# Non-local attention block: a fourth tile of each image turned by DMA, split by ScalarE and VectorE, and three operand moves made ScalarE copies

## The reference

```python
g     = (einsum('bchw,oc->bhwo', x, w_g) + b_g).reshape(B, N, 64)
theta = (einsum('bchw,oc->bhwo', x, w_theta) + b_theta).reshape(B, N, 64)
phi   = (einsum('bchw,oc->bohw', x, w_phi) + b_phi).reshape(B, 64, N)
att   = softmax(einsum('bnc,bcm->bnm', theta, phi), axis=-1)      # 1024 x 1024 per image
y     = einsum('bnm,bmc->bnc', att, g).reshape(B, H, W, 64)
out   = einsum('bhwc,oc->bohw', y, w_out) + b_out
inv   = bn_gamma / sqrt(bn_var + 1e-5)
return x + out * inv + (bn_beta - bn_mean * inv)
```

## Time and profile before

| | before |
|---|---|
| median of three runs | 206.3 us |
| the profiled execution: its own time | 205.01 us |
| its span | 203.2 us |
| granted TensorE clock over the span | 0.997 |
| share of the span busy: TensorE matmul | 96% |
| VectorE | 86% |
| GpSimd | 76% |
| ScalarE | 67% |
| share of the 16 DMA engines' time, SyncE's queue | 81.3% |

### The profile page before, as it was taken

The page is one execution under the profiler, slowest core; times in us unless marked ns, Lnnn a source line. Parts: engine busy times, 40 slices in busy tenths (PEclk is TensorE's granted clock), DMA queues, the critical chain, the costliest instruction groups (busy, mean ns, idle before and its releaser), DMA issues.

```text
span 203.2 us, 3990 instructions
## 1 busy us (share of the span) xinstructions
PE 195.2 (96%) x1100; PEld 133.6 (66%) x1100; DVE 174.8 (86%) x289; ACT 136.8 (67%) x245; POOL 154.2 (76%) x130
## 2 busy tenths in 40 slices
PE   7998899999999999999999999999999998999993
PEld 7485776587666857677566957677566956566551
DVE  0687989988997899978998899978998899989881
ACT  2679867767486766866577765866577675767731
POOL 2479579999778999699987999699988964954300
PEclk9999999999999999999999999999999999999998
DMA  5309946799999998899979998899988998848102
GB/s 154 98 7 225 240 85 117 167 248 185 188 219 250 222 169 221 187 224 187 233 159 259 230 191 194 168 249 203 198 180 182 226 169 182 132 81 155 52 3 103
DMA packets 59500, 35.28 MB, mean 174 GB/s; under 512 B 50400, under 2 KB 50912, under 8 KB 59488
## 3 DMA queue, kind: packets, MB, share of 16 engines
q1 hardware_dynamic: 59200, 35.01, 81.3%
q10 hardware_dynamic: 288, 0.14, 0.2%
HBM read 8.36 MB, written 4.23 MB: 62 GB/s over the span
## 4 chain that ended last, share of the span: by engine, by line
PE 71%; DVE 10%; DMA 5%; POOL 5%; SPq 4%; issue 3%; ACT 1%; ACTq 0%; DVEq 0%; POOLq 0%
PE ps_scores L757 21%; PE ps_flip L821 12%; PE ps_y L769 11%; PE ps_misc L783 6%; PE ps_y L776 5%; PE ps_misc L741 5%; DVE neg_max L622 4%; PE ps_misc L864 4%; DMA pt_hi<-p_hi 3%; DVE pt_lo L663 3%; SPq L302 2%; POOL p_lo L478 2%; DMA w_tp<-w_tp_t_dram 2%; PE ps_scores L795 1%; POOL x_lo L492 1%
## 5 line engine op out<-in xcount | busy, mean ns | idle before, releaser
L552 ACT ACTIVATE probs<-ps_scores,neg_max 128x1024 f32<-128x1024 f32 x64 | 71.7, 1120 | 29.1 <-DVE neg_max L627 14.9
L622 DVE TENSOR_REDUCE neg_max<-ps_scores 128x1 f32<-128x1024 f32 x64 | 77.9, 1217 | 9.5 <-PE ps_scores L757 9.1
L663 DVE SCALAR_TENSOR_TENSOR pt_lo<-ps_flip,pt_hi 128x512 f16<-128x512 f32 x84 | 54.0, 684 | 5.2 <-ACT pt_hi L539 5.1
L539 ACT ACTIVATE pt_hi<-ps_flip 128x512 f16<-128x512 f32 x84 | 45.6, 595 | 15.2 <-PE ps_flip L821 15.2
L478 POOL TENSOR_TENSOR p_lo<-probs,p_hi 128x1024 f16<-128x1024 f32 x22 | 47.0, 2139 | 4.7 <-POOL p_hi L471 3.9
L757 PE MATMUL ps_scores<-phi_hh,theta_hl 128*128 128x512 f32 x128 | 47.0, 448 | 0.8 <-ACT probs L552 0.6
L821 PE MATMUL ps_flip<-ident,probs 128*128 128x128 f32 x336 | 44.6, 275 | 1.8 <-DVE pt_lo L663 1.0
L821 PEld LDWEIGHTS ps_flip<-ident,probs 128*128 128x128 f32 x336 | 38.1, 142 | 11.1 <-issue 3.6
L757 PE MATMUL ps_scores<-phi_ll,theta_hl 128*128 128x512 f32 x128 | 40.1, 394 | 0.0
L769 PE MATMUL ps_y<-pt_hi,g_parts 128*128 128x512 f16 x120 | 28.4, 379 | 0.1
L757 PEld LDWEIGHTS ps_scores<-phi_ll,theta_hl 128*128 128x128 f32 x128 | 24.0, 188 | 5.6
(11 more groups left out here) (77 smaller groups left out, 173.8 us busy)
## 6 DMA issues: line engine op xcount, KB each, us to landing
x_in<-x_in_dram SPq DMA_DIRECT2D x16, 256.0 KB, 3.3
inv_all<-inv_row SPq DMA_DIRECT2D x15, 256.0 KB, 3.9
out_dram<-resid SPq DMA_DIRECT2D x15, 256.0 KB, 2.7
phi_hh<-hi SPq DMA_DIRECT2D x14, 256.0 KB, 5.7
phi_ll<-lo SPq DMA_DIRECT2D x14, 256.0 KB, 6.2
theta_hl<-hi SPq DMA_DIRECT2D x7, 256.0 KB, 4.7
theta_hl<-lo SPq DMA_DIRECT2D x7, 256.0 KB, 5.5
pt_hi<-p_hi SPq DMA_TRANSPOSE x22, 4.1
```

The lines of the kernel that those rows point to most:

```text
L539: nc.scalar.activation(pt_hi[ring][:, c * HALF_TILES:(c + 1) * HALF_TILES, slot * P:(slot + 1) * P], ps_flip[c][:, :].rearrange("p (a n) - ...
L552: nc.scalar.activation(probs[k % PROB_RING][:, :], ps_scores[k % 2][:, :], ACT.Exp, bias=neg_max[:, k % STEPS:k % STEPS + 1], accum_out=ro ...
L622: nc.vector.tensor_reduce(out=top, in_=ps_scores[k % 2][:, :], op=ALU.max, axis=AX.X, negate=True).then_inc(row_max_ready if by_dma(it, k) ...
L663: nc.vector.scalar_tensor_tensor(out=pt_lo[ring][where], in0=ps_flip[c][:, :].rearrange("p (a n) -> p a n", n=P), scalar=PROB_SCALE, in1=p ...
```

## The change

Tile 2 of every image goes by DMA as well. It does not take GpSimd: ScalarE writes its `p_hi` (`own_high`, in step 3, ahead of exp of tile 3) and VectorE its `p_lo` (`own_low`, in step 3, ahead of the maximum of tile 4). VectorE also adds log(2^15) to that tile's maximum. The reciprocals of the first half now have two scaled columns (places 1 and 2; in the first image 0 and 2). The three moves that keep their partitions become ScalarE copies of 64x1024 (`same_rows`, in steps 4, 6 and 7), counted by a new semaphore `copied`, for which scores of a new image and the overwrite of `hi` now wait.

```diff
-    STACKS = 6
+    STACKS = 3
+    COPIES = 3
+    COPY_STEPS = (4, 6, 7)
...
-    BY_DMA = (1, 5, 7)
+    BY_POOL = (1, 5, 7)
+    BY_ACT = 2
+    BY_DMA = (1, BY_ACT, 5, 7)
...
-    FIRST_BY_DMA = (0, 5, 7)
+    FIRST_BY_POOL = (0, 5, 7)
+    FIRST_BY_DMA = (0, BY_ACT, 5, 7)
...
                     sp.wait_ge(hi_ready, b + 1)
-                    restack(theta_hl[1 - r], 0, hi, 0, 1 - r)
                     restack(phi_hh[1 - r], 0, hi, CI, 1 - r)
-                    restack(phi_hh[1 - r], CI, hi, CI, 1 - r)
+                turn_hi(MT * b + BY_ACT)
+                if exists(b + 1, B):
                     sp.wait_ge(lo_ready, 2 * b + 2)
                     restack(theta_hl[1 - r], CI, lo, 0, 1 - r)
                     restack(phi_ll[1 - r], 0, lo, CI, 1 - r)
-                    restack(phi_ll[1 - r], CI, lo, CI, 1 - r)
...
                 turn_lo(MT * b + 1)
+                turn_lo(MT * b + BY_ACT)
...
+            def copy_rows(target, source, rows):
+                nc.scalar.activation(target[rows, :], source[rows, :].bitcast(F32), ACT.Copy).then_inc(copied, 1)
+
+            def same_rows(it, k):
...
+                if j == COPY_STEPS[0]:
+                    act.wait_ge(hi_ready, image + 1)
+                    copy_rows(phi_hh[ahead], hi, slice(CI, P))
+                if j == COPY_STEPS[1]:
+                    act.wait_ge(lo_ready, 2 * image + 2)
+                    copy_rows(phi_ll[ahead], lo, slice(CI, P))
+                if j == COPY_STEPS[2]:
+                    act.wait_ge(hi_ready, image + 1)
+                    copy_rows(theta_hl[ahead], hi, slice(0, CI))
+
+            def own_high(it, k):
+                t = tile_at(it, k)
+                if exists(t, TILES) and by_act(it, k):
+                    act.wait_ge(probs_ready, t + 1)
+                    wait(act, hi_moved[0], moved_by(it, k) - moved_each(k))
+                    nc.scalar.activation(p_hi[BY_ACT][:, :], probs[k % PROB_RING][:, :],
+                                         ACT.Copy).then_inc(own_hi_ready, 1)
...
+            def own_low(it, k):
+                t = tile_at(it, k)
+                if exists(t, TILES) and by_act(it, k):
+                    dve.wait_ge(own_hi_ready, image_at(it, k) + 1)
+                    wait(dve, lo_moved[0], moved_by(it, k) - moved_each(k))
+                    nc.vector.tensor_tensor(p_lo[BY_ACT][:, :], probs[k % PROB_RING][:, :], p_hi[BY_ACT][:, :],
+                                            ALU.subtract).then_inc(own_lo_ready, 1)
...
-                        slots = FIRST_BY_DMA[:1] if tile_is(it, k - 1, HALF_TILES - 1) else IN_HALF[ring_of(k - 1)]
-                        moved = inv_sum[:, cols.start + slots[0]:cols.start + slots[-1] + 1:2]
+                        slots = FIRST_BY_DMA[:2] if tile_is(it, k - 1, HALF_TILES - 1) else IN_HALF[ring_of(k - 1)]
+                        moved = inv_sum[:, cols.start + slots[0]:cols.start + slots[1] + 1:slots[1] - slots[0]]
...
+                own_low(it, k - 1)
                 low_parts(it, k)
...
                     pe.wait_ge(stacked[r], it * 16 * STACKS + 16 * STACKS * ((k // MT + 1) // 2))
+                    pe.wait_ge(copied, COPIES * image_at(it, k))
```

More of the change, by code:

```diff
@@ L148, in build_nonlocal_attention @@
         stacked = [sem(f"stacked{i}") for i in range(2)]
+        copied = sem("copied")
         stored = [sem(f"stored{i}") for i in range(2)]
@@ L188, in build_nonlocal_attention @@
         inv_in_row = sem("inv_in_row")
+        own_hi_ready = sem("own_hi_ready")
+        own_lo_ready = sem("own_lo_ready")
         row_max_ready = sem("row_max_ready")
@@ L244, in move_at, with split_at, by_act @@
             return counted(it, k, BY_DMA, FIRST_BY_DMA)
+        def split_at(it, k):
+            return counted(it, k, BY_POOL, FIRST_BY_POOL)
+        def by_act(it, k):
+            return k % MT == BY_ACT and by_dma(it, k)
         def home_of(it, k):
@@ L310, in turn_hi @@
                 wait(sp, y_ready, t // HALF_TILES - 1)
-                sp.wait_ge(p_hi_ready, move_at(0, t) + 1)
+                if by_act(0, t):
+                    sp.wait_ge(own_hi_ready, t // MT + 1)
+                else:
+                    sp.wait_ge(p_hi_ready, split_at(0, t) + 1)
                 sp.dma_start_transpose(pt_hi[ring][:, :, slot * P:(slot + 1) * P],
@@ L319, in turn_lo @@
                 ring, slot = ring_of(t), t % HALF_TILES
-                sp.wait_ge(p_lo_ready, move_at(0, t) + 1)
+                if by_act(0, t):
+                    sp.wait_ge(own_lo_ready, t // MT + 1)
+                else:
+                    sp.wait_ge(p_lo_ready, split_at(0, t) + 1)
                 sp.dma_start_transpose(pt_lo[ring][:, :, slot * P:(slot + 1) * P],
@@ L418, in step @@
                         hold(stacked[r], it * 16 * STACKS + 16 * STACKS * ((k // MT + 1) // 2))
+                        hold(copied, COPIES * b)
                     nc.gpsimd.tensor_scalar(out=hi[:, :], in0=qk[:, :], scalar1=1.0, scalar2=0.0,
@@ L433, in step @@
                                             scalar2=1.0, op0=ALU.mult, op1=ALU.mult).then_inc(probs_scaled, 1)
-                if exists(t, TILES) and by_dma(it, k - 1) and not tile_is(it, k, 1):
+                if exists(t, TILES) and by_dma(it, k - 1) and not by_act(it, k - 1) and not tile_is(it, k, 1):
                     tile_high(it, k - 1)
@@ L475, in tile_low @@
                 ring = ring_of(k)
-                hold(p_hi_ready, move_at(it, k) + 1)
+                hold(p_hi_ready, split_at(it, k) + 1)
                 hold(lo_moved[ring], moved_by(it, k) - moved_each(k))
@@ L542, in high_parts @@
                             ACT.Copy, scale=PROB_SCALE).then_inc(pt_hi_ready, 1)
+            def copy_rows(target, source, rows):
+                nc.scalar.activation(target[rows, :], source[rows, :].bitcast(F32), ACT.Copy).then_inc(copied, 1)
+            def same_rows(it, k):
+                image, j, ahead = image_at(it, k), k % MT, (k // MT + 1) % 2
+                if not exists(image + 1, B):
+                    return
+                if j == COPY_STEPS[0]:
[14 more added lines that the diff above has]
+                                         ACT.Copy).then_inc(own_hi_ready, 1)
             def exponential(it, k):
@@ L547, in exponential @@
                     act.wait_ge(max_ready, t + 1)
-                    if by_dma(it, k - PROB_RING):
-                        wait(act, p_lo_ready, move_at(it, k - PROB_RING) + 1)
+                    if by_act(it, k - PROB_RING):
+                        act.wait_ge(own_lo_ready, image_at(it, k - PROB_RING) + 1)
+                    elif by_dma(it, k - PROB_RING):
+                        wait(act, p_lo_ready, split_at(it, k - PROB_RING) + 1)
                     else:
@@ L571, in step @@
                     exponential(it, k)
+                own_high(it, k - 1)
+                same_rows(it, k)
                 high_parts(it, k)
```

## The result

The changed kernel takes 208.28 us (median of 6 runs, 207.94 to 210.66) against 205.56 us for the kernel before (6 runs, 204.61 to 206.87): a ratio of 1.0188 with a 95% interval of 1.0147 to 1.0229. By the ratio it is slower by about 3.9 us. The medians differ by only 2.7 us: three of the six runs of the kernel before (206.2 to 206.9) are those of the first table, and the ratio fits the other three (204.6 to 204.9). The ratios leave out runs over 1.5% above the fastest of their kernel. The profiled execution has a span of 206.4 us against 203.2. Where ratios of two sessions are compared, each has its own interval, 0.3 to 0.8 points either way; a point is 1% of the time of the kernel before.

What follows compares the result with a forecast made beforehand. TensorE was taken as the bound, VectorE close behind. Span 203.2 us, minus 8 x 0.91, plus the same 7.3 as waits, plus 0.2, gives 203.4; 205.2 with 1.8 around it; median 1.3 higher, 206.5; range 201.5 to 212.

Steps and rivals of the forecast that it cites:

- rival 1: First half's scaling misses the gap and stands 2.14 us behind GpSimd's `p_lo`; about 0.9 us per image stays; 211.5 us; chance 0.27.
- TensorE gives 7.3 us, all of it eaten by waits of VectorE for GpSimd.: One tile's flips, 0.91 us in each of 8 images, leave TensorE; the same 7.3 us returns as waits for VectorE.
- rival 3: TensorE stays the bound and all 7.3 us are kept: 199 us; chance 0.07.
- ScalarE: 19.4 us per image, copies at 1.12, hidden.: `p_hi` of tile 2 and three 64-row copies at 1.12 us each, costed at 0 ahead of exp's waits; under 22 us.
- Rival 4: ScalarE's copies of steps 6 and 7 delay `pt_hi` and the next image's scores; some 210 us; chance 0.12.
- DMA: 0.: Queue loses three moves, gains two transposes per image; taken as 0, with 1.7 us gain or loss as far ends.
- VectorE's own work: +0.15 us, the subtraction 1.2.: Per image, two `pt_lo` go, a 1.2 us subtraction and 0.15 us log term come; VectorE comes to 21.3 us.
- The subtraction behaves as the two-column scaling does.: VectorE's `p_lo` of tile 2 stands until GpSimd's running instruction ends; possible wait 0 to 2.14 us.
- The scaling slips into that gap by 0.07 us.: First half's two-column scaling, at 90.80, starts 0.07 us before GpSimd's `p_lo` at 90.87, in the gap after `p_hi`.
- The first image: 0.: The first image has much the same work on VectorE, so its change was taken as 0.
- The second half's scaling goes from 0.35 to 1.0 us.: Sign at the image's end: the two-column scaling stands behind the later `x_lo` until 102.8, giving back the 0.7 us lead.

## Why the prediction was wrong in its likeliest case

The range held the time, and the slower side had the largest chance, but the time written down, 206.5 us, was for no change. A range of 201.5 to 212 us takes in almost every rival, so that it held says little. That the time fell between the forecast and rival 1 (211.5) was in no case of the prediction: it is a mean over images that were struck and images that were not. By its own steps:

- *TensorE gives 7.3 us, all of it eaten by waits of VectorE for GpSimd.* Right in kind, too large in size. Without those waits the ratio is 0.977: 4.8 us, and 3.9 us of span. There TensorE is busy throughout the middle again, and one tile's flips are worth 0.7 us per image, not the 0.91 read from the chain. That is rival 3's condition, at a smaller gain. The waits then took back more than all of it: six images of the middle take 133.9 us without them and 140.2 with them.
- *ScalarE: 19.4 us per image, copies at 1.12, hidden.* Measured 19.5 and 19.9 us in full images, 1.04 to 1.07 a copy; 64 rows cost as much as 128. Hidden in the middle, as forecast, but not in the first image, where TensorE waits 1.55 us for the copy of step 7. Rival 4 had named this wait, for every image.
- *DMA: 0.* Right as the sum of both parts; no wait of `sum_high` for a transpose is left in the changed kernel. It hides a large term: with the extra transposes but all six moves on the queue, the kernel is 4.5 points slower.
- *VectorE's own work: +0.15 us, the subtraction 1.2.* Right: 1.21 where it did not wait. It was forecast to wait 0.3 us for GpSimd's `lo`; in the image shown it began just as `lo` ended (89.94 against 89.98), and the longest of its waits in the middle, 0.6 us, was for `p_hi`.
- *The subtraction behaves as the two-column scaling does.* Right, and shown by replacing it: GpSimd's `p_hi` late by 1.1 us, 3.1 points of time. The Trainium skill (SBUF — State Buffer, "SBUF: two separate sides") states that an instruction of VectorE in a two-port mode or with two SBUF inputs, and one of GpSimd, exclude each other for the whole instruction through a shared pair of ports. The traces agree in both directions: 2.10 us of scaling at 92.39 behind `p_lo`, 2.11 us of `p_hi` at 89.94 behind the subtraction. No row says which mode the scaling runs in.
- ***The scaling slips into that gap by 0.07 us.* This is the step that failed.** VectorE's side was exact: 1.24 us from the subtraction's end to the scaling, 1.26 forecast. GpSimd's was not: I let `p_hi` begin at the end of the subtraction's record, and it ended 0.90 us after that end (92.05 against 91.15), not 1.05. By its length of 1.05 us it had resumed some 0.15 us before the record of VectorE's instruction ended (an estimate; the other three such cases of the run give the same), so its `p_lo` began first. In three of the six images the scaling then took 2.1 us, in one 1.9, in two 0.8. Single columns in its place gave back 1.1 of the 1.9 points.
- *Rival 1, 0.9 us per image, 5.2 in all.* The mechanism came, and the size for an image that it strikes: 23.9, 24.1 and 23.9 us against 23.0. But the other three took 23.3 (with the scaling of 1.9 us), 22.9 and 22.3, and the mean is 0.4 us over six images. The term was mis-sized by taking one pattern for all images. What sets the pattern of an image was not traced.
- *The first image: 0.* It lost 0.7 us of the span's 3.2. The wait of TensorE for the copy of step 7 (1.55 us) lies in it. The kernel with all six moves as DMAs has no such wait, and makes the reciprocals of the first image's second half at 32.52 us, as the kernel before does (32.49). The same kernel with copies makes them at 34.75, the changed kernel at 34.00, and the kernel before with the copies alone at 33.45.
- *The second half's scaling goes from 0.35 to 1.0 us.* 0.99 at 104.63, but 0.17 to 0.75 in the other six. Single columns there gave another 1.1 points, on top of those of the first half.

Of the versions tried that compute the whole reference, the changed kernel with single-column scalings is the best (0.9965), and its interval (0.9928 to 1.0003) still includes no difference from the kernel before.

## What to carry to other kernels

A tiny instruction can be the dearest one: look at the longest and not only the mean duration of a group, since VectorE's waiting for GpSimd stands inside the busy time. Before moving element-wise work to VectorE beside a busy GpSimd, count which instructions could wait for it (here the subtraction with two SBUF inputs and the scaling of two columns), and where on GpSimd's timeline they will fall. When an outcome hangs on a margin as thin as the 0.07 us here, it has no likeliest case: give both prices equal weight, and do not expect every image to fall the same way.

## What the runs showed of the hardware that was not expected

- A scaling of one column never waited for GpSimd (0.14 to 0.16 us, 30 of 30 in one kernel), one of two columns did in 11 of the 15 cases of the changed kernel, for up to 1.9 us beyond its own 0.17. In the other four GpSimd ran nothing or had at most 0.14 us to go.
- GpSimd goes on some 0.15 us before VectorE's recorded end (estimated from four cases of the changed kernel, where `p_hi` ended 0.90 to 0.91 us after the subtraction and takes 1.05 by itself). With VectorE waiting, its scaling ends 0.01 to 0.04 us after GpSimd's instruction (94.49 after 94.47).
- Whoever waits goes on when the other's instruction ends, even between two consecutive instructions of the same engine: GpSimd's `p_hi` ran between the two pieces of 512 columns, and the second piece took 1.52 us in place of about 0.7. Splitting the subtraction cost a second wait.
- The profile shows such waits as longer instructions, never as idle time with a releaser: the list of waits of the changed kernel does not name one.
